# Latent contexts of two of four tiles in four 64x64 matmuls, and routing logits with the gate's weights stationary

## The reference, cut to what matters

```python
scores = jnp.einsum('bhsr,bhlr->bhsl', q_r, k_r)
attn = jax.nn.softmax(scores, axis=-1)
ctx_c = jnp.einsum('bhsl,bld->bhsd', attn, kv_r)
ctx_lat = jnp.einsum('bhsd,hkd->bhsk', ctx_c, w_kc_kv)
...
return ctx @ Wo.T
...
logits = x @ gate_weight.T
probs = jax.nn.softmax(logits.astype(jnp.float32), axis=-1).astype(logits.dtype)
topv, topi = jax.lax.top_k(probs, TOP_K)
```

## Time and profile before

| what | value |
| --- | --- |
| three runs, median (lowest to highest) | 850.51 us (849.42 to 851.28) |
| the profiled execution, its own time | 850.23 us |
| its span in the profile | 847.6 us |
| PE busy | 829.7 us, 98% |
| DVE, ACT, POOL busy | 633.2, 280.3, 180.9 us |

### The profile page before, as it was taken

The page is one execution under the profiler, slowest core; times in us unless marked ns, Lnnn a source line. Parts: engine busy times, 40 slices in busy tenths (PEclk is TensorE's granted clock), DMA queues, the critical chain, the costliest instruction groups (busy, mean ns, idle before and its releaser), DMA issues.

```text
span 847.6 us, 15993 instructions
## 1 busy us (share of the span) xinstructions
PE 829.7 (98%) x6350; PEld 668.7 (79%) x6350; DVE 633.2 (75%) x1392; ACT 280.3 (33%) x500; POOL 180.9 (21%) x152
## 2 busy tenths in 40 slices
PE   9999999999999999999999999999999999999996
PEld 7977678876887768776777888888888888888885
DVE  5587688899888998888867966666665766576576
ACT  5431353204432144302544423332322323232242
POOL 3046500563006630166412201200000000000121
PEclk9999999999999999999999999999999999999998
DMA  9300000100001000020120042201012020000001
GB/s 352 147 18 2 3 2 12 52 2 5 2 14 51 2 5 2 2 81 5 68 74 26 1 127 91 77 1 65 30 50 68 0 93 34 29 1 0 1 31 69
DMA packets 13091, 35.84 MB, mean 42 GB/s; under 512 B 1504, under 2 KB 2784, under 8 KB 12640
## 3 DMA queue, kind: packets, MB, share of 16 engines
q1 hardware_dynamic: 13024, 34.92, 11.9%
HBM read 30.26 MB, written 2.36 MB: 38 GB/s over the span
## 4 chain that ended last, share of the span: by engine, by line
PE 49%; DVE 2%; issue 1%; POOL 0%; ACT 0%; ACTq 0%; DVEq 0%
PE ps L256 15%; PE ps L258 15%; PE ps L257 15%; PE ps L1670 2%; PE ps L1661 1%; PE ps L638 1%; PE ps L1644 1%; PE ps L641 0%; PE ps L666 0%; DVE h_lo L371 0%; POOL roped L816 0%; PE ps L1564 0%; DVE su L539 0%; PE ps L1513 0%; PE ps L1506 0%
## 5 line engine op out<-in xcount | busy, mean ns | idle before, releaser
L816 POOL TENSOR_TENSOR roped<-prod 128x512 f32<-128x512 f32 x96 | 121.3, 1288 | 231.4 <-DVE prod L1150 231.3
L539 DVE TENSOR_TENSOR su<-sg,ps 128x512 f32<-128x512 f32 x96 | 66.0, 687 | 120.4 <-PE ps L258 118.2
L256 PE MATMUL ps<-y_hi,f_hi 128*128 128x512 f32 x384 | 151.2, 394 | 0.0
L258 PE MATMUL ps<-y_hi,f_lo 128*128 128x512 f32 x384 | 149.5, 389 | 0.0
L257 PE MATMUL ps<-y_lo,f_hi 128*128 128x512 f32 x384 | 149.4, 389 | 0.0
L400 ACT ACTIVATE sg<-ps 128x512 f32<-128x512 f32 x96 | 57.3, 598 | 251.3 <-PE ps L258 251.2
L1150 DVE TENSOR_TENSOR prod<-ps,ropeq 128x512 f32<-128x512 f32 x192 | 118.8, 682 | 23.9 <-PE ps L258 21.7
L257 PEld LDWEIGHTS ps<-y_lo,f_hi 128*128 128x128 f32 x384 | 72.1, 188 | 15.2 <-issue 0.5
L258 PEld LDWEIGHTS ps<-y_hi,f_lo 128*128 128x128 f32 x384 | 72.1, 188 | 15.2
L256 PEld LDWEIGHTS ps<-y_hi,f_hi 128*128 128x128 f32 x384 | 72.1, 188 | 15.1 <-issue 0.5
L256 PE MATMUL ps<-xT_hi,a_hi 128*128 128x512 f32 x192 | 78.8, 410 | 2.1 <-DVE prod L1150 2.1
(11 more groups left out here) (186 smaller groups left out, 1344.6 us busy)
## 6 DMA issues: line engine op xcount, KB each, us to landing
cb<-routing SPq DMA_DIRECT2D x32, 256.0 KB
f_raw<-in_L_ffn_gate_up_proj SPq DMA_DIRECT2D x8, 768.0 KB, 6.2
f_raw<-in_L_ffn_down_proj SPq DMA_DIRECT2D x8, 384.0 KB, 7.3
xb<-in_x SPq DMA_DIRECT2D x4, 512.0 KB, 4.1
lq<-in_L_xattn_Wq SPq DMA_DIRECT2D x1, 2048.0 KB, 14.3
x2T_all<-in_L_xattn_Wo SPq DMA_DIRECT2D x1, 2048.0 KB, 12.5
x2T_all<-x2T SPq DMA_DIRECT2D x4, 512.0 KB, 3.4
roped<-in_L_xattn_w_kc_q SPq DMA_DIRECT2D x1, 1536.0 KB, 10.0
```

Of the source, the lines that this page charges most:

```text
L256: pe.matmul(dst, l_hi, r_hi, start=first, stop=False, skip_group_check=check)
L258: return pe.matmul(dst, l_lo, r_hi, start=False, stop=last, skip_group_check=check)
L539: dve.tensor_tensor(su[:, k % 2], sg[:, k % 2], bank(2 * (k % 2) + 1), ALU.mult).then_inc(s_su, 1)
L816: pool.tensor_tensor(roped[:, 2 * (t % 4) + k], made(2 * t + k)[:, 0], made(2 * t + k)[:, 1], ALU.add)\
```

## The change

It has three parts. **(1)** For tiles 1 and 2 (`QUARTERED`) `context` becomes four matmuls of a 64x64 stationary block, 512 columns moving: for each half h of the key rows and each sequence `odd` one, into the rows 64*(h^odd) of bank 4+h. For this `scores` exchanges the two heads of a pair for the odd sequences of these tiles, and `bd` holds their blocks off the diagonal (`DIAGONALS`): `diagonal` takes three copies per half instead of one, on ACT and, for block 0, on POOL. ACT's `context` copies these tiles in four copies of 64 partitions instead of two of 128. **(2)** ACT's `diagonal` stands behind the two `xT_hi_out` instead of ahead of them. **(3)** `logits` has 32 columns of the gate stationary and 128 tokens moving, one column group of 32 per tile, into experts x tokens; ACT copies these rows (`logits_out`), PE turns them (`turn_logits`), and DVE reads them as before. In `pairs` the matmuls move to the middle of slot 2, the transpose stands at its end.

```diff
+    QUARTERED = (1, 2)
+    DIAGONALS = ((slice(0, 8, 2), 0), (slice(1, 8, 6), 0), (slice(3, 6, 2), 1))
-    LOGITS = ps[:, 7, 0:TILES * EXPERTS]
+    logits_bank = lambda b: 7 if b < BLOCKS - 1 else 4
+    logits_place = lambda b: ps[:, logits_bank(b), 0:TILES * EXPERTS]
+    logits_rows = rt[:, 2].rearrange("p t x -> p (t x)")
...
@@ ffn_scalar, step 5 of the first round @@
+                    logits_out(LAST)
                     y_hi_out(act, LAST)
@@ ffn_tensor, after ffn_up(5) and after dn(3) @@
+                    if first and k == LOGITS_STEP:
+                        logits(LAST)
...
-                    logits(LAST, LAST_LOGITS)
+                    turn_logits(LAST)
@@ gpsimd: diagonal(b) @@
-                if h:
-                    pool.wait_ge(s_bd, 2 * b + 1)
-                pool.tensor_tensor(bd[r, :, 64 * h:64 * h + 64], kv[r], kt[r], ALU.add).then_inc(s_bd, 1)
-            pool.wait_ge(s_bd, 2 * b + 2)
+                for i, (q, swap) in enumerate(DIAGONALS):
+                    o = 64 * (h ^ swap)
+                    if h or i:
+                        pool.wait_ge(s_bd, 6 * b + 3 * h + i)
+                    pool.tensor_tensor(bd[r, q, o:o + 64], kv[r, q], kt[r, q], ALU.add).then_inc(s_bd, 1)
+            pool.wait_ge(s_bd, 6 * b + 6)
@@ scalar @@
+        def logits_out(b):
+            if b:
+                act.wait_ge(s_c, b)
+            act.wait_ge(s_lgr, b + 1)
+            act.activation(logits_rows, ps[:, logits_bank(b), P:2 * P], ACT.Copy).then_inc(s_lgc, 1)
@@ scalar, pairs: ahead of squares(b + 1) @@
+            if later:
+                logits_out(b - 1)
@@ scalar, cross @@
-                    act.activation(ct[:, :, 64 * h:64 * h + 64], bank(4 + h).rearrange("p (r s) -> p r s", s=SEQ),
-                                   ACT.Copy).then_inc(s_ct, 1)
+                    if t in QUARTERED:
+                        for odd in range(2):
+                            r = slice(64 * (h ^ odd), 64 * (h ^ odd) + 64)
+                            ins = act.activation(ct[r, :, 64 * odd:64 * odd + 64],
+                                                 ps[r, 4 + h, :].rearrange("p (r s) -> p r s", s=SEQ), ACT.Copy)
+                        ins.then_inc(s_ct, 1)
...
-                    act.activation(bd[r, :, 64 * h:64 * h + 64], kt[r], ACT.Copy).then_inc(s_bd, 1)
+                    for q, swap in DIAGONALS:
+                        o = 64 * (h ^ swap)
+                        act.activation(bd[r, q, o:o + 64], kt[r, q], ACT.Copy).then_inc(s_bd, 1)
...
                 context(3)
-                diagonal()
                 xT_hi_out(n, 0, s_x1t, s_x1hi)
                 xT_hi_out(n, 1, s_x1t, s_x1hi)
+                diagonal()
@@ tensor @@
-            for t in range(TILES):
-                for kc in range(KC):
-                    mm = pe.matmul(place[:, t * EXPERTS:(t + 1) * EXPERTS], x2T[:, kc, t * P:(t + 1) * P],
-                                   gate_w[:, kc, :], start=kc == 0, stop=kc == KC - 1)
-            mm.then_inc(s_lg, 1)
+            for kc in range(KC):
+                for t in range(TILES):
+                    mm = pe.matmul(ps[32 * t:32 * t + 32, logits_bank(b), P:2 * P], gate_w[:, kc, :],
+                                   x2T[:, kc, t * P:(t + 1) * P], start=kc == 0, stop=kc == KC - 1)
+            mm.then_inc(s_lgr, 1)
+
+        def turn_logits(b):
+            pe.wait_ge(s_lgc, b + 1)
+            pe.transpose(logits_place(b), logits_rows, ident[:]).then_inc(s_lg, 1)
@@ tensor, scores @@
-                        o = 64 * p
+                        swap = odd if t in QUARTERED else 0
+                        o = 64 * (p ^ swap)
+                        keys = slice(64 * (r ^ swap), 64 * (r ^ swap) + 64)
                         mm = pe.matmul(ps[64 * odd:64 * odd + 64, score_bank(b) + r, o:o + 64], lq[i, p, c:c + 64],
-                                       bdT[i, 2 * t + odd, i], start=True, stop=True)
+                                       bdT[i, 2 * t + odd, keys], start=True, stop=True)
@@ tensor, pairs @@
                     mm.then_inc(s_q, 1)
+                    if later and t == 2 and k == 0:
+                        logits(b - 1)
...
                 if later and t == 2:
-                    logits(b - 1, LOGITS)
+                    turn_logits(b - 1)
@@ tensor, context @@
-                    pe.matmul(bank(4 + h), bd[:, 2 * t + h, :], at[:, t % 2, :, 64 * h:64 * h + 64],
-                              start=True, stop=True).then_inc(s_av, 1)
+                    if t in QUARTERED:
+                        i = slice(64 * h, 64 * h + 64)
+                        for odd in range(2):
+                            r = slice(64 * (h ^ odd), 64 * (h ^ odd) + 64)
+                            mm = pe.matmul(ps[r, 4 + h, :], bd[i, 2 * t + odd, r], at[i, t % 2, :, 64 * odd:64 * odd + 64],
+                                           start=True, stop=True)
+                        mm.then_inc(s_av, 1)
```

More of the change, by code:

```diff
@@ L183, in build @@
     a_psum = lambda k: ps[:, k % 4, 0:384].rearrange("p (r h c) -> p r h c", h=2, c=32)
-    LAST_LOGITS = ps[:, 4, 0:TILES * EXPERTS]
     s_ident, s_tables = sem("ident_loaded"), sem("tables_loaded")
@@ L217, in build @@
     s_x2t, s_x2T = sem("x2T_in_psum"), sem("x2T_ready")
-    s_lg = sem("logits_in_psum")
+    s_lgr, s_lgc, s_lg = sem("logit_rows_in_psum"), sem("logit_rows_copied"), sem("logits_in_psum")
     s_lsub, s_lexp, s_c = sem("logits_shifted"), sem("logits_exp_ready"), sem("routing_ready")
@@ L384, in final_sum, with ffn_scalar @@
         return ps[:, f:f + 2, :].rearrange("p k (t d) -> p (k t) d", d=D)
-    def ffn_scalar(act, x2T_out):
+    def ffn_scalar(act, x2T_out, logits_out):
         def body(it, first, last):
@@ L563, in body @@
                 if first and k == LOGITS_STEP + 1:
-                    shift_logits(LAST, LAST_LOGITS)
+                    shift_logits(LAST)
                 for part in range(6):
@@ L602, in ffn_up, with ffn_tensor @@
             mm.then_inc(s, 1)
-    def ffn_tensor(pe, turn_x2, logits):
+    def ffn_tensor(pe, turn_x2, logits, turn_logits):
         def body(it, first, last):
@@ L749, in next_kv @@
         def next_kv(b):
-            sp.wait_ge(s_bd, 2 * b + 2)
+            sp.wait_ge(s_bd, 6 * b + 6)
             load_kv(b + 1)
@@ L959, in context @@
                     act.wait_ge(s_av, 8 * b + 2 * t + h + 1)
-                    act.activation(ct[:, :, 64 * h:64 * h + 64], bank(4 + h).rearrange("p (r s) -> p r s", s=SEQ),
-                                   ACT.Copy).then_inc(s_ct, 1)
+                    if t in QUARTERED:
[4 more added lines that the diff above has]
+                        ins.then_inc(s_ct, 1)
+                    else:
+                        act.activation(ct[:, :, 64 * h:64 * h + 64], bank(4 + h).rearrange("p (r s) -> p r s", s=SEQ),
+                                       ACT.Copy).then_inc(s_ct, 1)
             xout = lambda t: x2T_out(b, t, 5)
@@ L1018, in _ @@
         over_blocks(linear, pairs, cross)
-        ffn_scalar(act, x2T_out)
+        ffn_scalar(act, x2T_out, logits_out)
     @block.vector
@@ L1157, in side @@
                 if later and t == 2 and i == 3:
-                    shift_logits(b - 1, LOGITS)
+                    shift_logits(b - 1)
                 if following and t == 4 and i == 3:
@@ L1256, in red, with shift_logits @@
             own.step(dve.tensor_reduce(o, x, AX, op))
-        def shift_logits(b, place):
-            lg = place.rearrange("p (t x) -> p t x", x=EXPERTS)
+        def shift_logits(b):
+            lg = logits_place(b).rearrange("p (t x) -> p t x", x=EXPERTS)
             dve.wait_ge(s_lg, b + 1)
@@ L1442, in turn_kv @@
         def turn_kv(b, i, f):
-            pe.wait_ge(s_bd, 2 * b + 2)
+            pe.wait_ge(s_bd, 6 * b + 6)
             for q in range(4 * i, 4 * i + 4):
@@ L1499, in turn_x2, with logits @@
             mm.then_inc(s_x2t, 1)
-        def logits(b, place):
+        def logits(b):
             pe.wait_ge(s_x2T, 4 * b + 4)
-            for t in range(TILES):
-                for kc in range(KC):
-                    mm = pe.matmul(place[:, t * EXPERTS:(t + 1) * EXPERTS], x2T[:, kc, t * P:(t + 1) * P],
-                                   gate_w[:, kc, :], start=kc == 0, stop=kc == KC - 1)
-            mm.then_inc(s_lg, 1)
+            for kc in range(KC):
[6 more added lines that the diff above has]
+            pe.transpose(logits_place(b), logits_rows, ident[:]).then_inc(s_lg, 1)
         def keep_warm(n, f=0):
@@ L1660, in context @@
                         pe.wait_ge(s_ct, 8 * b + 2 * t)
-                    pe.matmul(bank(4 + h), bd[:, 2 * t + h, :], at[:, t % 2, :, 64 * h:64 * h + 64],
-                              start=True, stop=True).then_inc(s_av, 1)
+                    if t in QUARTERED:
[5 more added lines that the diff above has]
+                        mm.then_inc(s_av, 1)
+                    else:
```

(4 more changed lines are left out.)

## The result

| what | before | after |
| --- | --- | --- |
| median (lowest to highest), 4 runs each, compared side by side | 849.96 us (849.31 to 851.28) | 843.53 us (843.40 to 844.17) |
| ratio, 95% interval | | 0.9929 (0.9918 to 0.9941) |
| span of the profiled execution | 847.6 us | 841.7 us |
| PE busy | 829.7 us | 821.1 us |

The kernel is 6.0 us faster by the ratio (5.0 to 7.0), 6.4 by the medians, 5.9 by the spans. The forecast of 843.5 us was met to the tenth, but its working was not: it took 7.0 us off a median of 850.51, and the kernel before has since measured 849.6 to 850.0 in larger groups of runs. Of the promised gain 0.6 us are missing by the medians and 1.0 by the ratio. The point was met by luck: a base some 0.6 us too high met a gain that was too large by as much.

What follows compares the result with a forecast made beforehand. PE, busy 829.7 of 847.6 us, was taken as the bound. Contexts 2.4 (blocks 0 to 2) and 1.15 (block 3) plus logits 3.45 make 7.0 us off the 850.51 median: 843.5 us, range 840.5 to 848.5.

Steps and rivals of the forecast that it cites:

- all four tiles of the array run at once: Contexts of tiles 1 and 2 on PE: 1.1 us instead of 1.72, saving 0.62 each in eight places.
- (b): PE's packs: only two tiles overlap, a context takes 1.72 + 0.25 us; 851.8 us in all, chance 0.06.
- (c): PE's contexts: tiles with 512 moving columns run one after the other, 3.44 + 0.25 us; 862.8 us, chance 0.04.
- the logits: Logits on PE: 0.68 us plus 0.11 transpose instead of 1.70; 2.55 kept in three blocks, 0.9 in expert loop.
- just in time: DVE ahead of slot 3 in pairs: free at 161.0, PE delivers at 160.98, so 0.85 us is kept.
- the diagonal is hidden: ACT's six diagonal copies take 1.7 us, end at 146.4, 1.0 us ahead of turn_kv on PE.
- tile 2 in blocks 0 to 2: xout(0) waits 0.4 to 0.45 us for ACT's four copies; of 1.24 us a block keeps 0.8, together 2.4.
- The sign to look for: PE in the profile after: 0.4 us idle ahead of xout(0) would show the forecast right.
- block 3: Contexts 1 and 2 there: project(1) loses 0.1 us at most, nothing lost behind context 2; 1.15 us kept.
- The sum: Whole kernel: 2.4 + 1.15 + 3.45 = 7.0 us saved, forecast 843.5 us.
- Rival (a): ACT's copies set the pace, one every 0.86 us, four in 3.2; only 2.5 us saved, 848.0 us, chance 0.13.

Runs made afterwards that it cites:

- the last experiment: One of tile 1's four copies in block 3 moved from ACT to DVE, against the kernel with turn(3) ahead and tile 3 quartered in block 3: 840.84 us, ratio 0.9897.
- the experiment: Two unread ACT copies added ahead of the last copy in tile 2's context, against the changed kernel: 846.67 us; in tile 1's instead: 844.64 us.

## Why the prediction came out as it did

**Right: all four tiles of the array run at once.** A context in quarters takes 1.05 us to the next start, forecast 1.1. Rivals (b), near 2 us, and (c), near 3.7, are out. On the Trainium skill's rule of strict program order (TensorE: Matmul & The Clock Gate, Part 3) the trace shows that it does not stop four tiles from overlapping, each with two records.

**Right: the logits.** 0.87 saved on PE (forecast 0.9), 0.82 kept per stage in pairs and 0.83 in the loop (0.85 and 0.9), 3.3 us by these rows and 3.6 by the run with the logits alone (3.45). DVE was "just in time", as said: it is now the other bound of slot 3. The transpose costs the 0.11 forecast: 0.03 to the next start (157.24 to 157.27) and 0.08 in the step behind that (157.27 to 157.58, 0.31 instead of 0.23).

**Right: the diagonal is hidden.** Six copies in 1.64 us (forecast 1.7), 1.1 us to spare (1.0). The order of ACT's work around it is worth nothing either way.

**Mis-sized: tile 2 in blocks 0 to 2.** The step said 2.05 us for four copies (one every 0.48, as the full-height ones of the earlier trace rows), with `xout(0)` late by 0.4 to 0.45, and 0.8 of 1.24 kept per block: 0.62 of tile 1 and 0.2 of tile 2. Measured: 2.28 us, `xout(0)` 0.55 late, and 1.63 us kept in three blocks instead of 2.4. Tile 1 gave its 0.65 per block. The whole of the missing part is tile 2's, which costs 0.1 per block instead of giving 0.2. Its rows add up. The context saves 0.67 (1.72 to 1.05). PE takes 0.09 more on the way into it (the group ahead of it takes 1.87 us instead of 1.78 with no context in quarters) and 0.08 more behind it (`self_context`, 1.86 instead of 1.78). The wait is 0.55, and after it the two matmuls of `xout` take 0.27 to the next start instead of 0.22. So 0.67 - 0.09 - 0.08 - 0.55 - 0.05 = -0.1. The step had nothing for the way in and out beyond the context itself, and nothing for the restart, and its wait was 0.13 too short. (The sign to look for, 0.4 us of idle PE ahead of `xout(0)`, is met by the bracket of 0.39, but only because the bracket shows too little.)

The copies' pace of 0.48 was right for copies of the same rows and wrong for two of the three steps, at which the rows change: 0.60, 0.50, 0.59. That makes the four 0.23 us longer. They began 0.1 earlier than forecast and so ended 0.11 later (131.96 against 131.85).

**Mis-sized: block 3.** The step said that `project(1)` would be 0.1 late and block 3 would keep 1.15: 0.52 at `project(1)` and 0.62 at context 2. `project(1)` was due at 418.68 (417.75 and the 0.93 that the turn takes there in the earlier trace rows) and came at 419.25, 0.57 late. The copies are 0.23 longer; and the due time was earlier, since a 64x64 context followed by `scores`, which is 64x64 too, takes only 0.91 (415.80 to 416.71), where the full one took 1.88. That helped the due time and not the start. From context 1 to `project(1)` 0.45 is kept (3.90 us before, 3.45 after). `project(1)` then took 3.65 to context 2 instead of 3.46, and this 0.19 the step did not have. About 0.09 of it is the way into context 2: with tile 2 only, where `project(1)` waits for nothing, it takes 3.55 (421.83 to 425.38). The other 0.10 comes with the wait: `project(3)` with all four tiles, late as well but with a full-array group behind it, takes 3.56 (143.64 to 147.20). Context 2 and the step behind it save 0.58. Kept: 0.45 - 0.19 + 0.58, with rounding 0.86.

**The sum.** Contexts 2.5 by rows and 2.8 by the run of their own, for 3.55; logits 3.3 by rows and 3.6 by run, for 3.45. The cause, ACT's copies that PE waits for, was named and had the right sign in both places. Two things were left out: what PE pays at the edges of small tiles and after a wait, and what ACT pays when the rows change. The second stood in the rows: the two half-height copies of the earlier trace rows, the second with the other rows, took 1.27 us together, where two full-height ones behind them took 1.09.

**Rival (a)** had the right mechanism with too high a price: copies one every 0.86 would have given 848.0, and they came one every 0.56 in the mean. The Trainium skill's section PSUM Bottleneck (TensorEngine Tiling (Array Packing)) is borne out here in kind: with tiling PE waits for the copies out of PSUM in four places, 0.55 us or a little more each, and the gain of tile 2 in blocks 0 to 2 is gone. The same section's advice to use both ScalarE and VectorE brought 0.4 to 0.7 us in the last experiment.

**Why four copies take 2.28 us.** Each lasts 0.58 to 0.59, as long as a full-height one (0.60), so neither the height nor the strided target makes one longer. The start of the next is what differs. In every quartered context of every profile here the step is 0.48 to 0.50 us where the next copy has the same rows and 0.58 to 0.61 where it has the other half of them. The two added copies of the experiment show it best: they have the rows of the copy ahead of them and another target, and start 0.48 behind it and behind each other; the real copy behind them has the other rows, and starts 0.60 later. Full-height copies came 0.48 apart.

**Open.** Why a change of rows costs ACT 0.11 us. Copying both results' rows 0 to 63 first and then both results' rows 64 to 127 would have one change of rows instead of two; by these steps that is an estimated 0.1 us per context. It was not tried.

## To carry to other kernels

A product in quarters of the array cuts PE's time, but it makes more copies that can all start only at its end: count the time from there to the first instruction that needs the bank or the copy, and put work that needs neither in between. Put groups of the same small tiles behind each other, and copies of the same rows too. The best test was to do one tile alone, since tile 1 gave nearly all and tile 2 nothing, though both contexts were as short on PE. What a group gains is read at the next start that another engine gates, not from its own length.

## What was not expected of the hardware

- Going in and out of small tiles has its own price, which start-to-start of the group alone does not show. On the way in it is 0.09 us: the 0.23 us step of the 512-column matmuls becomes 0.32 ahead of the logits (154.85 to 155.17), and `project` takes 3.55 instead of 3.46 ahead of a context in quarters. On the way out it is 0.11 to 0.14: the context takes 1.02 to 1.05 us in front of a full-array group and 0.91 in front of `scores`, which has 64x64 tiles too, for 0.86 of matmuls. The step of 0.33 right behind the logits (155.75 to 156.08) is none of it, since it is 0.31 to 0.32 behind full-array groups as well (157.27 to 157.58; behind the logits before, 158.77 to 159.09). The Trainium skill (TensorEngine Tiling (Array Packing), Key Properties) says that a change of tiling mode drains TensorE; the rows agree in that each change costs about 0.1 us, and cannot show a drain as such.
- A wait costs PE a little beyond itself: `xout` takes 0.27 instead of 0.22 to the next start, `project` 3.56 instead of 3.46.
- A copy of 64 partitions by 512 columns out of PSUM takes ACT as long as one of 128 (0.59 and 0.60), and it starts 0.48 to 0.50 behind a copy of the same rows but 0.60 behind one of the other half. Two halves cost more than twice one in a piece.
- The idle time that a view shows ahead of a group of matmuls can be too small by the overhang of the modelled end before it: 0.39 shown at `xout(0)`, 0.55 by the starts.
